# Projection of both sample halves side by side on 64 rows each, with its bias written into the PSUM banks beforehand

## The reference, cut to what matters

```python
e = jnp.stack([tbl_0[ids[:, 0]], ..., tbl_25[ids[:, 25]]], axis=1)
x = layer_norm(dense_t @ Wd.T, gd, bd)
y = layer_norm(jnp.einsum('bnd,ed->bne', sparse_t, Ws), gs, bs)
y = jnp.einsum('bne,pn->bep', y, Wsi)
y = layer_norm(y, gsi, bsi)
y = jnp.swapaxes(y, 1, 2)
T = jnp.concatenate([x[:, None, :], y], axis=1)
Z = jnp.einsum('bnd,bmd->bnm', T, T)
...
h = jnp.maximum(h @ W_top1 + b_top1, 0.0)
h = jnp.maximum(h @ W_top2 + b_top2, 0.0)
y = h @ W_top3
```

## Time and profile before

| what | us |
|---|---|
| median of 3 runs (193.14 to 194.11) | 193.77 |
| the profiled execution, its own time | 194.12 |
| its span, first to last instruction | 192.2 |
| busy: PE 148.4, POOL 101.6, DVE 99.7, ACT 89.6 | |
| mean granted TensorE clock, share of full | 0.964 |

### The profile page before, as it was taken

One profiled execution on the slowest core, in us unless ns is written; L12 is line 12 of the kernel. 1 busy time (PEld: TensorE's weight loads), 2 busy tenths in 40 slices (PEclk: granted clock), 3 DMA queues, 4 the chain that ended last, 5 costly groups with the idle time before them and its releaser, 6 DMA issues.

```text
span 192.2 us, 4178 instructions
## 1 busy us (share of the span) xinstructions
PE 148.4 (77%) x1644; PEld 96.9 (50%) x1644; DVE 99.7 (52%) x192; ACT 89.6 (47%) x225; POOL 101.6 (53%) x113
## 2 busy tenths in 40 slices
PE   0496496958767976488869867798695889989995
PEld 0343444534444643354457646455565566446674
DVE  2390946684916882838073847361838456541001
ACT  3613043744512566755545436436744546641251
POOL 4777364757874487676375774776757720000000
PEclk9999669999979999969999999999999999999999
DMA  5813131416311015431011155111011640025000
GB/s 143 272 30 76 34 110 26 127 26 211 116 28 22 10 27 129 72 55 27 9 21 20 30 139 80 31 34 20 20 24 27 156 66 3 3 65 106 6 3 0
DMA packets 20260, 11.58 MB, mean 60 GB/s; under 512 B 12945, under 2 KB 17681, under 8 KB 20242
## 3 DMA queue, kind: packets, MB, share of 16 engines
q1 hardware_dynamic: 16226, 7.83, 15.2%
q0 software_dynamic: 3328, 3.41, 10.0%
q10 hardware_dynamic: 688, 0.08, 0.3%
HBM read 9.15 MB, written 2.16 MB: 59 GB/s over the span
## 4 chain that ended last, share of the span: by engine, by line
PE 40%; POOL 20%; DMA 13%; DVE 11%; issue 9%; ACT 5%; SPq 1%; POOLq 1%; DVEq 0%; ACTq 0%
POOL e_rows L373 20%; DMA e_rows<-table_dram,rows_sb 7%; PE mix_ps L440 7%; PE o_ps L488 5%; PE quad_ps L451 5%; PE proj_ps L474 4%; DMA dense_sb<-dense_t_dram 3%; DVE e_unit L910 3%; DVE e_prod L882 3%; DVE var_n L885 3%; PE dots_ps L465 3%; PE turn_ps L432 2%; PE o_ps L403 2%; PE dots_ps L396 2%; PE o_turn_ps L403 2%
## 5 line engine op out<-in xcount | busy, mean ns | idle before, releaser
L373 POOL DMA_INDIRECT e_rows<-table_dram,rows_sb x104 | 100.7, 968 | 53.1 <-issue 27.7
L440 PE MATMUL mix_ps<-mixw_sb,e_unit 128*128 128x192 f32 (+4 forms) x128 | 23.0, 325 | 17.0 <-DVE e_unit L910 17.0
L440 PEld LDWEIGHTS mix_ps<-mixw_sb,e_unit 128*128 128x128 f32 x128 | 20.0, 199 | 25.6 <-DVE e_unit L910 25.6
L882 DVE TENSOR_TENSOR e_prod<-quad_ps,e_rows 128x384 f32<-128x384 f32 (+1 forms) x16 | 9.5, 591 | 45.2 <-PE quad_ps L451 45.2
L474 PE MATMUL proj_ps<-f_sb,proj_w 128*128 128x512 f32 x60 | 32.5, 625 | 0.0
L873 DVE TENSOR_REDUCE var_p<-y_sq 128x16 f32<-128x512 f32 x32 | 20.5, 677 | 1.6 <-ACT y_sq L665 1.6
L451 PEld LDWEIGHTS quad_ps<-gram,e_cols 128*128 128x128 f32 x104 | 14.5, 206 | 12.2 <-ACT e_cols L673 11.2
L680 ACT COPY f_sb<-mix_ps 64x512 f32<-64x512 f32 x32 | 18.5, 578 | 4.5 <-PE mix_ps L440 4.1
L665 ACT ACTIVATE y_sq<-proj_ps 128x512 f32<-128x512 f32 x30 | 17.7, 589 | 5.9 <-PE proj_ps L474 5.7
L432 PE MATMUL turn_ps<-small_sb,e_rows 128*128 128x128 f32 x52 | 9.7, 302 | 13.9 <-DMA e_rows<-table_dram,rows_sb 13.8
L897 DVE TENSOR_TENSOR feats<-proj_ps,rstd_p 128x512 f32<-128x512 f32 x30 | 19.3, 686 | 0.6
(11 more groups left out here) (142 smaller groups left out, 172.8 us busy)
## 6 DMA issues: line engine op xcount, KB each, us to landing
z_dram<-z_mine SPq DMA_DIRECT2D x4, 512.0 KB, 3.2
e_rows<-table_dram,rows_sb POOLq DMA_INDIRECT x104, 2.5
w_sb<-w_dram SPq DMA_DIRECT2D x2, 512.0 KB, 6.6
wl_sb<-wl_dram SPq DMA_DIRECT2D x2, 512.0 KB, 3.4
w_sb<-w_dram SPq DMA_DIRECT2D x1, 768.0 KB, 4.2
dense_sb<-dense_t_dram SPq DMA_DIRECT2D x1, 512.0 KB, 5.8
wl_sb<-wl_dram SPq DMA_DIRECT2D x1, 256.0 KB, 2.7
z_pairs<-z_dram SPq DMA_DIRECT2D x4, 64.0 KB, 2.0
```

The costliest lines, as they stand in the source:

```text
L373: pool.indirect_dma_start(out=e_rows[:, chunk, t, D * ab:D * (ab + 1)], out_offset=None, in_=table, in_offset=bass.IndirectOffsetOnAxis(ap ...
L440: mm = pe.matmul(mix_ps[:, PR * at:PR * (at + number)], e_unit[:, t, :], mixw_sb[:, t, lo:lo + number, :].rearrange("k b p -> k (b p)"), s ...
```

## The change

- ACT `save_f` is one copy of 128 rows: both halves go to f_sb in the rows in which mix_ps has them. The rows 64 to 127 of f_sb written once ahead are gone.
- proj_w holds the projection's 64 rows twice, in rows 0 to 63 and in rows 64 to 127. `project` is two matmuls behind each other, half 0 on rows 0 to 63 and half 1 on rows 64 to 127, into the two banks. Both stand ahead of quad(i); the place behind quad(i) is empty.
- The matmuls add to what lies in the banks (`start=False`). What lies there is y_seed, the bias spread over the samples: for slot 0 it is put in by PE (two matmuls with the identity), for the others by ACT in `seed(i)`, two copies of 128x512 from SBUF to PSUM. Each waits for the norm_p instruction of slot i-1 that reads its bank, and both are waited for by project(i).
- seed(i) stands in ACT's round i >= 1 behind save_f(i) and the tower's steps and ahead of save_z(i-2).
- The last slot's projection goes to proj_ps too; project(15) moves behind dots(14), and seed(15) goes between save_f(15) and square(15, 0).
- Ahead of the loop, four ACT copies of 64x512 become one ACTIVATE of 128x512, one small copy and one POOL memset go.

```diff
-            def project(s, ab):
+            def project(s):
                 _, q = place(s)
-                if s < SLOTS - 1:
-                    wait(pe, y_ready, 2 * s - 1 + ab)
-                pe.wait_ge(f_ready, 2 * s + ab + 1)
-                pe.matmul(proj_of(s, ab), proj_w[:], f_sb[:, q % 2, ab, :], start=True,
-                          stop=True).then_inc(projected, 1)
+                pe.wait_ge(f_ready, s + 1)
+                if s == 0:
+                    pe.wait_ge(prep_act, 7)
+                    for ab in range(2):
+                        pe.matmul(proj_ps[:, ab, :], eye_sb, y_seed[:], start=True, stop=True)
+                wait(pe, seeded, 2 * s)
+                for ab in range(2):
+                    half = slice(D * ab, D * (ab + 1))
+                    pe.matmul(proj_ps[:, ab, :], proj_w[half, :], f_sb[half, q % 2, :], start=False, stop=True,
+                              skip_group_check=True).then_inc(projected, 1)
...
                 turn(i)
                 if i >= 1:
-                    project(i - 1, 0)
+                    project(i - 1)
                 quad(i)
-                if i >= 1:
-                    project(i - 1, 1)
...
-            project(last, 0)
-            project(last, 1)
             dots(last - 1)
+            project(last)
...
-                for ab in range(2):
-                    act.copy(f_sb[0:D, q % 2, ab, :], mix_ps[D * ab:D * (ab + 1), :]).then_inc(f_ready, 1)
+                act.copy(f_sb[:, q % 2, :], mix_ps[:]).then_inc(f_ready, 1)
+
+            def seed(s):
+
+                for ab in range(2):
+                    act.wait_ge(y_ready, 2 * (s - 1) + ab + 1)
+                    act.copy(proj_ps[:, ab, :], y_seed[:]).then_inc(seeded, 1)
...
+                if i >= 1:
+                    seed(i)
                 if 2 <= i < SLOTS - 2:
                     save_z(i - 2)
...
             save_f(last)
+            seed(last)
             square(last, 0)
```

More of the change, by code:

```diff
@@ L110 @@
 PACK = {}
-for _name, _width in (("eye", P), ("ws", EW), ("wsi", PR), ("gs", 1), ("gd", 1), ("bd", 1),
+for _name, _width in (("eye", P), ("ws", EW), ("wsi", PR), ("gs", 1), ("bs", 1), ("gd", 1), ("bd", 1),
                       ("gl", USED // P), ("bl", USED // P), ("b1", H1 // P), ("b2", H2 // P), ("w3", H2 // P)):
@@ L168, in tower @@
         rstd_n = sb("rstd_n", [P, 8])
-        f_sb = sb("f_sb", [P, 2, 2, 512])
+        f_sb = sb("f_sb", [P, 2, 512])
+        y_seed = sb("y_seed", [P, 512])
         y_sq = sb("y_sq", [P, 2 * QB, PR])
@@ L201, in tower @@
         ws_rows = sb("ws_rows", [EW, 2, D])
-        ws_grows = sb("ws_grows", [EW, D])
+        ws_grows = sb("ws_grows", [EW, 2, D])
         gram = sb("gram", [P, P])
@@ L241, in tower @@
             sem(n) for n in ("mixed", "f_ready", "projected", "sq_ready", "ssq_ready", "stdp_ready"))
-        y_ready, x_placed, dotted, z_saved, z_moved = (
-            sem(n) for n in ("y_ready", "x_placed", "dotted", "z_saved", "z_moved"))
+        y_ready, seeded, x_placed, dotted, z_saved, z_moved = (
+            sem(n) for n in ("y_ready", "seeded", "x_placed", "dotted", "z_saved", "z_moved"))
         z_last_in = [sem(f"z_last_in{t}") for t in range(KZ)]
@@ L281, in o_turned_to @@
             return o_turn_ps[:, P * j:P * (j + 1)]
-        def proj_of(s, ab):
-            return proj_last_ps[ab] if s == SLOTS - 1 else proj_ps[:, ab, :]
         def samples(chunk):
@@ L354, in _ @@
             pool.memset(gram[:], 0.0).then_inc(consts, 1)
-            pool.memset(proj_w[:], 0.0).then_inc(consts, 1)
             pool.memset(feats[:, :, :, 0], 1.0).then_inc(consts, 1)
@@ L380, in _ @@
             pe.wait_ge(small_in, 16)
-            pe.wait_ge(consts, 5)
+            pe.wait_ge(consts, 4)
             pe.wait_ge(prep_dve, 2)
@@ L437, in mix @@
                 pe.wait_ge(unit_ready, s + 1)
-                wait(pe, f_ready, 2 * s)
+                wait(pe, f_ready, s)
                 for n, (t, lo, at, number) in enumerate(mix_parts(q)):
@@ L601, in _ @@
             turn(last)
-            project(last - 1, 0)
+            project(last - 1)
             quad(last)
-            project(last - 1, 1)
             dots(last - 2)
@@ L630, in _ @@
         def _(act):
-            act.wait_ge(consts, 5)
+            act.wait_ge(consts, 4)
             act.activation(x_std[:, 0:1], eps[:, 0:1], ACT.Sqrt)
@@ L634, in _ @@
             act.wait_ge(prep_pe, 1)
-            for half in range(2):
-                for ab in range(2):
-                    last = act.copy(f_sb[D:P, half, ab, :].rearrange("p (b q) -> p b q", q=PR),
-                                    quad_ps[D:P, 0:PR].unsqueeze(1).to_broadcast([P - D, QB, PR]))
-            last.then_inc(prep_act, 1)
+            act.activation(y_seed[:].rearrange("p (b q) -> p b q", q=PR), quad_ps[:, 0:PR].unsqueeze(1).to_broadcast([P, QB, PR]),
+                           ACT.Copy, scale=bs_sb[:, 0:1]).then_inc(prep_act, 1)
             act.wait_ge(prep_pe, 2)
             act.copy(ws_rows[:], turn_ps[:, 0:D].unsqueeze(1).to_broadcast([P, 2, D])).then_inc(prep_act, 1)
-            act.activation(ws_grows[:], turn_ps[:, 0:D], ACT.Copy, scale=gs_sb[:, 0:1]).then_inc(prep_act, 1)
+            act.activation(ws_grows[:], turn_ps[:, 0:D].unsqueeze(1).to_broadcast([P, 2, D]), ACT.Copy,
+                           scale=gs_sb[:, 0:1]).then_inc(prep_act, 1)
             act.wait_ge(prep_pe, 3)
@@ L648, in _ @@
             act.wait_ge(prep_pe, 4)
-            act.copy(proj_w[D:D + 1, :], ws_sb[D:D + 1, :])
-            act.copy(proj_w[0:D, :], o_turn_ps[0:D, 0:EW]).then_inc(prep_act, 1)
+            act.copy(proj_w[:], o_turn_ps[:, 0:EW]).then_inc(prep_act, 1)
             act.wait_ge(prep_pe, 5)
@@ L665, in square @@
                 act.activation(y_sq[:, QB * ab:QB * (ab + 1), :].rearrange("p b q -> p (b q)"),
-                               proj_of(s, ab), ACT.Square).then_inc(sq_ready, 1)
+                               proj_ps[:, ab, :], ACT.Square).then_inc(sq_ready, 1)
             def save_cols(s):
@@ L1037 @@
     put("eye", np.eye(P, dtype=np.float32))
-    put("ws", np.concatenate([a["L0_rec_Ws"].T, a["L0_rec_bs"][None]]))
+    put("ws", a["L0_rec_Ws"].T)
     put("wsi", a["L0_rec_Wsi"].T)
     put("gs", columns(a["L0_rec_gs"]))
+    put("bs", columns(a["L0_rec_bs"]))
     put("gd", columns(a["L0_rec_gd"]))
```

7 lines of the change are left out of this document (3 added, 4 removed).

## The result

The changed kernel takes 210.65 us (median of 4 runs, 207.91 to 213.49) beside 193.94 for the kernel before on the same chip (193.14 to 196.0): ratio 1.076, 95% interval 1.061 to 1.091. The forecast was 201.3 with a range to 206.5. The direction was right, and the loss is twice the forecast one, 16.7 us instead of 7.5. Ratios here leave disturbed runs of either kernel out, so one can differ from that of the two medians beside it. The profiled execution took 213.13 us, at a mean granted clock of 0.903; the others had 0.919 to 0.950, so what its clock shows is the far end of the spread.

A forecast was written before the change was run, and what follows sets the result against it. It took the middle of the kernel to be bound by a loop of PE's dots and POOL's gathers. Its terms summed to 7.5 us on the profiled 194.12, so 201.6, or 201.3 as median, with an 8-in-10 range of 197.0 to 206.5.

The forecast's parts named there:

- The passes side by side: The two projection halves on different rows run at once, taking 0.87 us as one half did, so quad isn't moved.
- The seeds: ACT's two 128x512 copies into PSUM per slot, taken at 1.19 us a pair.
- The identity matmuls in round 1: Four passes on PE ahead of project(0) and quad(1), 1.72 us less 0.12 of slack: 1.6 us on the path.
- Round 2: seed(1) stands ahead of save_cols(2) on ACT and delays project(1) and quad(2): 1.6 us.
- Round 12: seed(11) stands ahead of save_cols(12), for which quad waits: 1.2 us.
- Round 8: seed(7) stands ahead of save_z and save_cols(8), for which quad(8) waits: 1.2 us.
- Switching between 128 and 64 rows: Cost of the array's change of row count around the pair: 0.02 us a round, 0.15 in all with rounding.
- the row of dots: Trace row where dots starts at 118.99, before the tower's last matmul ends at 119.07; read as showing no switch wait.
- Nothing: Rounds 3, 6, 9, 13: seeds end at most 0.2 us after project could start, rounds off the chain, no cost.
- the tail: After the last slot's save_f, seeds and dots(14) delay the last pair and the squares: 0.95 us.
- one more such stretch, at 1.4, is as likely as one fewer: Half-clock stretches of TensorE: one more, costing 1.4 us, was held as likely as one fewer, so no net cost.
- the rival in which the clock gives everything back: If TensorE's clock never fell, 7.7 us would return: 193.6, no change; chance 0.08, including anything else with that effect.

The follow-up runs named there:

- e1: The changed kernel without seed copies, identity matmuls and bias, the pair of projections starting its banks anew; 201.49 us, ratio 1.057.
- e5: The changed kernel with unused 512-column filler matmuls in nearly all of PE's waits; 201.47 us, ratio 1.052, at full clock.
- e6: e3 with each project contracting 64 rows instead of 128 at its old places, bias left out; 191.97 us in its one execution at full clock, others up to 201.64.
- e3: The kernel before with unused filler matmuls of ones by dense_sb in some of PE's waits; 190.46 us, ratio 0.993.
- e9: The changed kernel with e5's filler but without seeds, identity matmuls and bias; 195.6 us, span 193.3.
- e8: The changed kernel with pair, identity matmuls and seeds moved behind quad and save_cols, root_n ahead of both squares, plus filler; 194.19 us, ratio 1.014.
- e10: The kernel before with e3's filler, both projections behind quad and root_n ahead of the squares; 193.24 us, ratio 1.010.
- e7: e3 with eleven more small matmuls of ones ahead of the first long ones; 192.01 us, ratio 1.000.
- e11: The kernel before with both projections behind quad and root_n ahead of the squares, without filler; 201.8 us, ratio 1.046.

## Why the prediction was half right

The direction held, and the mechanism that the sum prices, seeds and identity matmuls ahead of quad, is there. Two terms of the sum were too small (the switch, and the rounds between 4 and 12), which makes 10.1 at full clock instead of 7.5. That alone would have stayed in the stated range (193.94 and 10.1 are 204.0). What carried the time beyond 206.5 is a term that the sum put at nothing, the clock.

**Held.** The passes side by side: four in 1.13. The seeds: 0.59 each, 1.19 a pair forecast, 1.10 to 1.19 seen. The identity matmuls in round 1: T to Q there is 3.20, and 1.48 in e1 without them, so 1.7 where 1.6 was forecast. Round 2: T to Q 3.09 against 1.48 without seeds, 1.6 as forecast. Round 12 with e5's clock: 2.86 against 1.64 in e1, 1.2 as forecast. Round 8: 3.44 against 2.04, 1.4 where 1.2 was forecast. PE's wait for e_unit went from 17.0 to 27.5.

**Failed: the step "Switching between 128 and 64 rows".** It took 0.02 a round and 0.15 in all, from the row of dots. e6 puts the price at 0.3 ahead of quad and 0.1 behind it, in each round, and some 1.3 us over that kernel. The row of dots was also misread. It says that dots starts at 118.99, ahead of the last tower matmul's end at 119.07, but ends of matmuls are modelled in the trace and overlap all the time. Starts tell more. Eight passes of the tower in e5, first with a matmul on all rows and columns behind them, then with dots:

```profile
117.29 1.06 PE L535 MATMUL o_turn_ps<-h_sb,w_sb 128*128 128x128 f32 x8
118.18 1.02 PE L446 MATMUL mix_ps<-dense_sb,ones 128*128 128x512 f32 x2
...
121.05 1.06 PE L535 MATMUL o_turn_ps<-h_sb,w_sb 128*128 128x128 f32 x8
122.04 0.77 PE L468 MATMUL dots_ps<-feats 128*32 128x33 f32 x64
```

The first follows in 0.89, dots in 0.99, and in the row of the prediction it is 0.98 as well. So dots pays 0.1 at its start, as the pair does: from turn's first pass the pair starts at 0.48 where one half started at 0.39. The row that was held against a switch price has it in it. The Trainium skill (TensorEngine Tiling (Array Packing), Key Properties) says that changing the tiling mode drains the engine, and the estimate from it was 2.2. By that rule the trace agrees, for 64 rows (e6) and for dots' 32 columns.

**Failed: which rounds are on the chain.** The sum took the chain of before, rounds 1, 2, 8 and 12 with gathers between them, and put "Nothing" beside 3, 6, 9 and 13. The two kernels at full clock show it stretch by stretch (e5 less e3, from the table of e9):

| us | forecast | measured |
|---|---|---|
| up to turn(4): rounds 1 and 2 | 3.2 | 1.75 |
| turn(4) to turn(8): rounds 5 and 7 | 0.8 | 2.1 |
| turn(8) to turn(12): round 8 | 1.2 | 3.5 |
| turn(12) to turn(15): round 12 | 1.2 | 1.0 |
| turn(15) to the end | 0.95 | 1.7 |
| switching | 0.15 | in the rows above |
| sum | 7.5 | 10.1 |

Rounds 1 and 2 lose what was forecast and the switch (quad(2) is 3.85 later in e5), but at full clock the gathers for slot 4 have slack, which takes up half of it. From round 4 on it is the other way: the rounds that had waited for gathers now last as long as the gathers, so seeds and switches in rounds 5, 6 and 7 count (T to Q 2.40, 2.64 and 3.30 in e5, 1.2 in e3; 0.24 of the 2.40 is e5's own filler), and 8 to 12 pay the seeds of round 8, 1.4, and the switch in each round, 0.4, which leaves some 0.5 of the 3.5 unexplained. The sum had the seeds end at most 0.2 behind the time at which project could start in rounds 3, 6, 9 and 13. In the changed kernel the pair waits 1.44 for them in round 3 and 0.88 in round 6, since each seed waits for a norm_p that hangs on the pair before it, so a delay is handed from slot to slot. POOL's share of the chain fell from 20% to 8%.

**Near in size, wrong reason: the tail.** Forecast 0.95, 1.7 by the table, of which 0.4 are the switch in round 15. From mix(15) to the first norm_p(15) it went from 6.33 to 7.33. But e1, without seeds, has that same 1.0: it comes from the last pair, which shares its banks with norm_p(14) and stands behind dots(14), where before it had banks of its own.

**Failed: "one more such stretch, at 1.4, is as likely as one fewer".** The price nearly held. 54 executions of the kernel before, put in order by their mean granted clock, show it:

| mean clock | 0.982 | 0.973 | 0.964 | 0.955, 0.956 | 0.947 | 0.938, 0.939 |
|---|---|---|---|---|---|---|
| executions | 2 | 12 | 12 | 19 | 4 | 5 |
| mean us | 190.3 | 191.3 | 193.1 | 194.3 | 195.1 | 196.6 |

Between 0.973 and 0.939 lie four stretches of 3.4 us and 5.3 us of time, 1.3 each. What failed is the likelihood: the changed kernel's profiled execution had the equivalent of eight more, and even its best clock, 0.950, is below the median of before. Ahead of three of its falls, at 33.4, 84.6 and 146.0, PE had waited for e_unit or for the seeds:

```profile
33.13 2.24 PE L436 MATMUL mix_ps<-mixw_sb,e_unit 128*128 128x128 f32 x8 [2.40 <-DVE e_unit L913]
...
83.86 1.84 PE L436 MATMUL mix_ps<-mixw_sb,e_unit 128*128 128x96 f32 x8 [2.40 <-DVE e_unit L913]
...
145.83 1.92 PE L476 MATMUL proj_ps<-f_sb,proj_w 64*128 64x512 f32 x4 [1.58 <-ACT proj_ps L680]
```

The prediction saw the mechanism (it wrote that the change "takes 0.87 of work a round from PE and lengthens its waits") and used it only against the rival in which the clock gives everything back. It should have been a rival of its own on the slow side. In figures: the medians differ by 16.7 us, those of e5 and e3 by 11.0, so 5.7 are the clock's, on top of the 3 that the kernel before loses to it; by the ratios (1.076, and 1.052 over 0.993) it is 3 rather than 6. The two ways leave 3 to 6. Filler in PE's waits raised the mean clock in each pair that differs by it (e3, e5, e8 and e10), so the clock does hang on those waits. It isn't enough to fill some of them: e7 has e3's filler and fell three times behind its start. Why a given wait is followed by a fall and a like one isn't was not settled: waits as long stand in the kernel before without one, and e11 shows that the pattern turns on small shifts.

## What to carry to other kernels

Work that fills an accumulator ahead of a matmul belongs to the place where the matmul's own engine is waiting anyway: the same seeds and pair made the kernel 17 us slower ahead of quad and 1 to 4 behind it. A matmul on half the rows between matmuls on all rows has a price even when two of them run side by side, so count the switches on the chain. And where PE waits a lot at a clock that falls now and then, a forecast needs a line for the clock on the slow side, and an experiment needs a pair of kernels with the waits filled (e3 and e5) before a difference is put down to anything else.

## What the runs showed of the hardware

- Matmuls on rows 0 to 63 and 64 to 127 with 512 columns run at the same time: four 32-bit passes in 1.13 us, two on all rows in 1.02.
- Going from 128 rows to 64 and back costs 0.2 us by the start of the next matmul (1.06 instead of 0.86, e6), and about 0.4 over the round. Going from 128 columns to 32 costs 0.1 by the start of dots (0.99 instead of 0.89 behind eight short passes, e5).
- ScalarE writes PSUM from SBUF as fast as SBUF from PSUM: 0.589 us for 128x512, beside 0.581 for save_f's copy.
- One order of instructions, with and without idle-time matmuls, differs by 7.7 us of span through the granted clock (e10, e11); one execution in 23 of a kernel was granted 0.56 of the clock from 13.7 us to nearly its end, and took 256.86 us instead of 190.65.
